# Count matrix of a four-layer graph network: 50 ranges of 50 destinations in place of 40 of 64, and an edge search in 28 places of 21 ranges

## The reference

```python
dst = min((2500 * uniform(40000) ** 2.0).astype(int32), 19999)   # then sorted, src with it
x = x + L0(h, ..., src, dst)                  # softmax over the edges into a node, sum of alpha * h[src]
W = zeros((256, 256)).at[rows, cols].set(w)   # L1: X @ W; rows = src, cols = dst, the last edge wins
agg = segment_sum(x[src], dst)                # L2: mean over neighbours, three times
x = x + L3(h, edge_index, W, a)
```

## Time and profile before

| | |
|---|---|
| median of 3 runs | 2108.89 us (2108.01 to 2110.15) |
| the profiled execution | 2108.91 us |
| its span | 2107.1 us |
| PE, DVE, ACT, POOL busy | 82%, 75%, 65%, 13% |
| block of the count matrix, first `ohc` to last `ohl` | 35.6 to 313.0 us |

### The profile page before, as it was taken

How to read it: one execution, slowest core, us unless ns; L and a number is a source line. 1 busy time by engine, 2 the same in 40 slices (tenths; PEclk the granted TensorE clock), 3 DMA queues, 4 the chain that set the end, 5 groups by cost and what they waited for, 6 DMA issues and landing times. The chain is left out here.

```text
span 2107.1 us, 63497 instructions
## 1 busy us (share of the span) xinstructions
PE 1724.7 (82%) x21987; PEld 1375.5 (65%) x21987; DVE 1575.6 (75%) x3485; ACT 1379.3 (65%) x2350; POOL 274.3 (13%) x421
## 2 busy tenths in 40 slices
PE   3999995598999748899893699998989985588883
PEld 1333333598888627889882477775558984588883
DVE  6999997899999888999999532222332257899996
ACT  0246794999999659999995622221113355799986
POOL 2466510366700000000000000000000000000000
PEclk9999997799999978999996899999999998799997
DMA  2000000011101000010101200000001010000002
GB/s 77 12 1 2 2 3 27 14 31 37 40 27 40 2 27 30 28 40 28 40 28 50 97 2 0 0 0 7 0 16 40 20 61 14 8 27 21 21 21 99
DMA packets 34789, 54.87 MB, mean 26 GB/s; under 512 B 10668, under 2 KB 26240, under 8 KB 34432
## 3 DMA queue, kind: packets, MB, share of 16 engines
q1 hardware_dynamic: 31232, 51.64, 7.5%
q0 software_dynamic: 3328, 0.06, 0.1%
HBM read 43.19 MB, written 8.49 MB: 25 GB/s over the span
## 5 line engine op out<-in xcount | busy, mean ns | idle before, releaser
L1069 ACT ACTIVATE Rm<-rows,cB 128x1280 bf16<-128x1280 f32 (+3 forms) x816 | 847.1, 1132 | 32.4 <-DVE Mn L1104 19.2
L1206 PE MATMUL ps<-R,M 128*128 128x132 f16 (+1 forms) x8640 | 684.1, 221 | 117.3 <-DVE Mn L1104 62.7
L1206 PEld LDWEIGHTS ps<-R,M 128*128 128x128 f16 x8640 | 545.4, 97 | 141.6 <-DVE M L1114 51.8
L1114 DVE TENSOR_TENSOR M<-Rm,C 128x1280 f16<-128x1280 bf16 (+3 forms) x816 | 527.9, 673 | 37.0 <-ACT Rm L1069 26.6
L1199 PE MATMUL ps<-HB,C 128*128 128x66 f16 x6400 | 304.2, 194 | 60.5 <-DVEq L1095 60.5
L1199 PEld LDWEIGHTS ps<-HB,C 128*128 128x128 f16 x6400 | 258.9, 98 | 60.7 <-DVEq L1095 60.7
L600 PE MATMUL acc<-ohc,ohl 128*128 128x420 f16 (+1 forms) x1161 | 246.0, 348 | 27.1 <-DVE ohl L564 23.9
L562 DVE TENSOR_SCALAR ohc<-cells,near 128x1280 f16<-128x1280 f16 x387 | 214.7, 555 | 27.9 <-PE acc L600 23.5
L1117 DVE SCALAR_TENSOR_TENSOR M<-rows,cN,C 128x1280 f16<-128x1280 f32 (+1 forms) x144 | 217.2, 1508 | 0.0
L600 PEld LDWEIGHTS acc<-ohc,ohl 128*128 128x128 f16 x1161 | 89.6, 98 | 175.6 <-DVE ohl L564 120.0
L1543 PE MATMUL psA<-R,C 128*128 128x512 f16 (+1 forms) x800 | 145.6, 332 | 8.1 <-DVEq L1827 3.2
(11 more groups left out here) (295 smaller groups left out, 2304.9 us busy)
## 6 DMA issues: line engine op xcount, KB each, us to landing
rows<-rowd SPq DMA_DIRECT2D x32, 640.0 KB, 3.9
rows<-rowd SPq DMA_DIRECT2D x16, 320.0 KB, 3.4
xd<-R SPq DMA_DIRECT2D x4, 640.0 KB, 2.9
xr<-xd SPq DMA_DIRECT2D x20, 128.0 KB, 2.1
xd<-HB SPq DMA_DIRECT2D x1, 2560.0 KB
xr<-xd SPq DMA_DIRECT2D x5, 512.0 KB, 6.4
R<-in_x SPq DMA_DIRECT2D x1, 2432.0 KB
xr<-in_x SPq DMA_DIRECT2D x19, 128.0 KB, 2.0
```

Source lines behind the costliest of these rows:

```text
L1069: a.activation(Rm[:, s % SG, 0:wide(p)], rows[:, p % 2, 0:wide(p)], ACT.Relu, bias=cB[:, ds(h + s * nh, 1)]).then_inc(s_R, 1)
L1114: v.tensor_tensor(M[:, u, 0:wide(p)], Rm[:, u, 0:wide(p)], Cs, ALU.min).then_inc(s_M if s in ONE else s_cut, 1)
L1206: m = pe.matmul(region(p % 2, r), lhsT, rhs, start=split and opens and r % 3 == 0, stop=True, skip_group_check=True)
```

## The change

- 50 ranges of 50 destinations (1000 cells). The banks are two of 500 columns. Destinations 2500 to 2559 belong to no range; POOL sets them to zero in the first block.
- A range's first two chunks (AHEAD) stand straight in the code, and the loop of threes comes behind them, with at least one turn. A range thus has 5, 8, 11, ... chunks in place of 6, 9, 12, ...; the ring's slot for a chunk is (2q + u) mod 3.
- The codes are shifted for two ranges at once (NEAR): `cells` has 2000 numbers, and an odd range compares with the second 1000.
- The search is in 28 places (NS): two one behind the other in each of ranges 0 to 6 and one in each of ranges 7 to 20, on PE after the two straight chunks. The number of searches at one place comes from the table (`turns`), up to 3.
- The chunks with dst < 256 are now taken from the first 6 ranges, thus up to destination 300.

```diff
-WW = 64
-NW = NP // WW
+WW = 50
+NW = -(-N // WW)
 U3 = 3
+AHEAD = 2
+NEAR = 2
...
+SEARCHED = [2] * 7 + [1] * 14
+NS = sum(SEARCHED)
+TURNS = -(-RND // NS)
...
-        DSPLIT = [(0, 22), (22, 43), (43, 64)]
-        cells = sb("cells", [P, CELLS], f16, edge)
+        DSPLIT = [(0, 25), (25, 50)]
+        cells = sb("cells", [P, NEAR * CELLS], f16, edge)
...
+                g.memset(C[:, :].rearrange("p (s d) -> p s d", d=NP)[:, :, NW * WW:NP], 0.0).then_inc(s_xz, 1)
...
-                ch(v.tensor_scalar(threes, threes, 1 / U3, 1 / U3, ALU.mult, ALU.add))
+                ch(v.tensor_scalar(threes, threes, 1 / U3, (1 - AHEAD) / U3, ALU.mult, ALU.add))
...
-                WT = D // WW
+                WT = -(-D // WW)
...
-                ch(v.tensor_scalar(table[:, T + 5:T + 6], many, 2.0 / NW, 0.5 - 1.0 / NW, ALU.mult, ALU.add))
+                ch(v.tensor_scalar(table[:, T + 5:T + 6], many, 2.0 / NS, 0.5 - 1.0 / NS, ALU.mult, ALU.add))
...
-                for q in range(NW):
+                for q in range(NS):
                     w = q % 2
                     with sp.Fori(0, turns) as i:
                         r = round_of(sp, q, i)
...
+                for q in range(NW):
+                    for c in searched(q):
+                        search(c)
...
-                    if q + 2 < NW:
-                        close_codes(q + 2)
+                    if q % NEAR == NEAR - 1 and q // NEAR + 2 < GROUPS:
+                        close_codes(q // NEAR + 2)
...
-                    v.wait_ge(s_near, q + 1)
+                    v.wait_ge(s_near, q // NEAR + 1)
+                    own = cells[:, q % NEAR * CELLS:(q % NEAR + 1) * CELLS]
+
+                    def one(i, u):
+                        k, w = chunk(first + i * U3 + u, NG * P - 1), slot_of(q, u)
+                        v.wait_ge(s_used, (before + i) * U3 + (q * AHEAD + u + 1))
+                        v.tensor_scalar(ohc[:, w, :], own, near[:, q // NEAR % 2, ds(k, 1)], None,
+                                        ALU.is_equal).then_inc(s_oh, 1)
...
+                    for u in range(AHEAD):
+                        one(0, u)
                     with v.Fori(0, threes) as i:
-                        for u in range(U3):
...
+                        for u in range(AHEAD, AHEAD + U3):
+                            one(i, u)
...
-                    three(0, True)
...
+                    for u in range(AHEAD):
+                        one(0, u, u == 0)
+                    for c in searched(q):
+                        search(c)
+                    with pe.Fori(0, threes) as i:
+                        for u in range(AHEAD, AHEAD + U3):
+                            one(i, u)
```

More of the change, by code:

```diff
@@ L117, in build @@
         hmax = sb("hmax", [P, NT], f32)
-        table = sb("table", [1, 4 * NW + 12], i32)
+        table = sb("table", [1, ROUNDS + TURNS * NS], i32)
         wd = nc.dram_tensor("wd", [D * D, 1], f32, kind="Internal").ap()
@@ L385, in _ @@
                 ch.wait()
[L386 to L388 removed]
+                for i in range(TURNS):
+                    ch(v.tensor_scalar(each[:, i, :], row[:, 4, 0:NS], turns, float(i), ALU.mult, ALU.add))
                 ch.wait()
[L390 removed]
+                ch(v.tensor_scalar(each[:, :, :], each[:, :, :], r1, r0, ALU.min, ALU.add))
                 ch.wait()
[L392 removed]
+                ch(v.tensor_copy(table[:, ROUNDS:ROUNDS + TURNS * NS].rearrange("a (i q) -> a i q", i=TURNS), each[:, :, :]))
                 ch(v.tensor_tensor(table[:, T + 3:T + 4], e0, some, ALU.add))
@@ L479, in threes_of, with slot_of, searched @@
             def threes_of(entry):
-                return nc.s_assert_within(entry // PACK, 2, NCH, skip_runtime_bounds_check_because=
-                                          "the table is built with at least two threes, and no more than cover NCH chunks")
+                return nc.s_assert_within(entry // PACK, 1, NCH, skip_runtime_bounds_check_because=
+                                          "the table is built with at least one three, and no more than cover NCH chunks")
+            def slot_of(q, u):
+                return (q * AHEAD + u) % U3
+            def searched(q):
+                return range(sum(SEARCHED[:q]), sum(SEARCHED[:q + 1]))
             @block.gpsimd
@@ L528, in _, with search @@
                 done = 0
-                for q in range(NW):
+                def search(c):
                     with a.Fori(0, turns) as i:
-                        n = turns * q + i
+                        n = turns * c + i
                         found = nc.s_assert_within(e0 + n * 4, 0, 8 * RND - 4, skip_runtime_bounds_check_because=
@@ L587, in _, with search @@
                 coming, before = packed(pe, 0), 0
+                def search(c):
+                    with pe.Fori(0, turns) as i:
+                        n = turns * c + i
+                        pe.wait_ge(s_sq, n + 1)
+                        hold(pe, s_row[c % 2], turns * (c // 2 * 48) + i * 48 + 48)
+                        pe.matmul(psD[c % 2][:, :], big16[:, :], notlater[:, :, :].rearrange("p u j -> p (u j)"),
+                                  start=True, stop=False)
+                        pe.matmul(psD[c % 2][:, :], left[:, c % 2, :], right[:, c % 2, :], start=False,
+                                  stop=True).then_inc(s_D, 1)
                 for q in range(NW):
@@ L591, in _ @@
                         coming = packed(pe, q + 1)
[L593 to L602, removed]
@@ L614, in _, with one @@
-                    with pe.Fori(1, threes) as i:
-                        three(i, False)
+                    def one(i, u, opening=False):
+                        w = slot_of(q, u)
+                        pe.wait_ge(s_oh, (before + i) * (2 * U3) + ((q * AHEAD + u) * 2 + 2))
+                        for b, (d0, d1) in enumerate(DSPLIT):
+                            if opening:
+                                pe.wait_ge(s_out, q * NB + b + 1)
+                            ins = pe.matmul(bank(b, q % 2), ohl[:, w, :], ohc[:, w, d0 * NT:d1 * NT],
+                                            start=opening, stop=True, skip_group_check=True)
+                        ins.then_inc(s_used, 1)
```

33 lines of the change are left out of this document (16 added, 17 removed).

## The result

The changed kernel takes 2124.19 us (median, 2123.39 to 2125.59) beside 2109.52 (2108.01 to 2110.49) of the kernel before, measured with it: a ratio of 1.0068 [1.0056, 1.0081], **14.7 us slower**. The forecast of 2119 had the direction, and the range from 2106 to 2129 holds the time. Two terms of its sum were wrong, and a gain was missing from it. The profiled execution has a span of 2122.0 us, 14.9 over the 2107.1 of before, so the two traces can be laid side by side.

A forecast was written before the change was run, and what follows sets the result against it. DVE's chunks were taken to set the pace of the count-matrix block. On 2108.9 us, -19.4 + 5.0 - 2.9 + 25.2 + 2.1 + 0.3 = +10.3 gave 2119 us; forecast's own range 2112 to 2126, wider range 2106 to 2129.

The forecast's parts named there:

- Shorter compare: DVE's compare on 1000 columns: 0.553 us a chunk for 403 chunks, against 0.626 for 387; -19.4 us.
- Range ends: DVE's pause at each range's end: 49 instead of 39, kept at 0.5 us each (bounds 0.1 and 0.65); +5.0 us.
- hidden by the straight chunks: Rival: two straight chunks fill DVE's queue before the loop, range-end pause shrinks to 0.1 us; 2099.5 us, chance 0.08.
- Single searches: DVE's pause behind a lone PE search: 13 of 0.47 us in place of 20 of 0.45; -2.9 us.
- Double searches: Ranges 0 to 6: PE waits 2.4 us for the second search's rows, DVE pauses 3.6 us; +25.2 us.
- The rival that the clock falls: PE's clock drops to 1.2 GHz in its 2.4 us pauses, adding some 25 us: 2144 us, chance 0.08.
- ACT: ACT is freed in ranges 21 to 49 and its shifts halved, but it hardly held DVE's pace; 0 us.
- First block: POOL's longer patterns, zeros and table rows delay PE's first transposes; +2.1 us (0.5 to 3).
- Scatters: POOL's later scatters, 48 in place of 40, stay hidden except beside a full DVE; +0.3 us (0 to 2).

The follow-up runs named there:

- e10_old_40: Kernel before (40 ranges of 64, one search in each), but each range's first three chunks stand straight, with the loop behind the search: 2103.61 us, ratio 0.9965.
- e1_spread: Changed kernel with one search in each of ranges 0 to 27 instead of two in 0 to 6 and one in 7 to 20: 2094.00 us, ratio 0.9925.
- e3_warm: Changed kernel with six extra PE matmuls, their results overwritten, between the two searches of ranges 0 to 6: 2115.41 us, ratio 1.0025.
- e2_ahead: Changed kernel, but SP loads a search's rows once the search before the last has ended, not the last one: 2109.62 us, ratio 0.9992.
- e4_load_late: Changed kernel, but DVE loads the next range's table entry after its two straight chunks, not ahead of them: 2116.94 us, ratio 1.0029.

## Why the prediction was right in direction and short in size

1. *Shorter compare*, -19.4: right. 0.5535 us a chunk against 0.553 forecast, -18.9 in all. The slope between two forms of one operation was a good price.
2. *Range ends*, +5.0: wrong by 5.5 us. The step was "I keep 0.5, since the load of the entry and the first address stay". They stay, but the branch into the loop leaves, and an end costs 0.37 over the pace as the mean, in e10_old_40 0.35 with nothing else changed. I had read this in the order of the instructions and given it no price. The truth lay between the bounds 0.1 and 0.65, and the rival "hidden by the straight chunks" (0.1) was no nearer than my 0.5.
3. *Single searches*, -2.9: e1_spread bears out that a single search costs little: ranges 0 to 6 lose 8.8 us for seven of them and the start of the block. The term itself was not measured apart.
4. *Double searches*, +25.2, of which the share over single searches was 3.1 each or 22: measured 34.2 in the ranges concerned, 28 to 30 in the whole time. The gap's 2.4 us was right to a tenth. "The pause is 0.47 + 2.4 + 0.7 = 3.6" failed, since it let PE go on at full speed behind the gap. The pauses are 4.1 to 4.75 us, and the chunks behind them are slow. Where e3_warm keeps the clock up, the pause is 3.4 to 3.7 over the pace and a double search costs 3.2 more than a single one: both as forecast, so the wait was priced well and the clock was what it lacked. The rival that the clock falls had the mechanism, and the earlier trace rows showed its level; I gave it 0.08 with the argument that 2.4 us is short beside the 12 in that row. It is not exclusive of the forecast, as I had it, but adds to it: 9 to 11 us, not the 25 that I gave it. The Trainium skill, "TensorE: Matmul & The Clock Gate", section "Part 1: The HAM clock gate", says that an idle array goes back to half its clock; the 0.53 of this trace from 123 to 126 us agrees. The row of before had the lower level behind 12 us of standing, and could not tell what 2.4 us would do.
5. *ACT*, 0: nothing contradicts it. In e2_ahead, once the rows are there, ACT's square is what ends the gap.
6. *First block*, +2.1: 1.7 measured. The memset is 1.13 us and the longer pattern 0.60 more.
7. *Scatters*, +0.3: not told apart; the rest of the program moved by less than its own spread.
8. *Missing from the sum:* the handover to the next block, -3.5. I looked at the searches only where they stand in PE's way and not at who waits for the last of them. The last ranges still had their searches before, the one that ends at 299 among them; POOL's last operation waited for the last of all, and DVE's 4.25 us behind the block was in the trace, unread.

The sum with the measured sizes: -18.9 - 0.5 + 34.2 + 1.7 - 3.5 = +13.0, and +1.9 in the rest. The Trainium skill, "DMA: Bandwidth & Descriptors", section "Anatomy of one DMA — SWDGE (gpsimd) path", fits about 2.0 us of fixed cost, for transfers that GpSimd issues. Carried over to SP's, it would have given a gap of 3.0; the trace has 2.34 to 2.81, so here the lower figure from the rows was the better one. The errors (+5.5 too dear, 3.5 missed, 12 too cheap) partly made up for each other, which is why 2119 looks better than its steps.

Where does the gain of the shorter compare go, then? Not into contention, and not off the critical path: the runs show that it is there (e1_spread, 2094.0). The seven double searches take it and 11 us more. The runs let the cost be divided, by what ranges 1 to 6 lose over the chunks' pace in each trace, as the mean of a range: 6.0 in the changed kernel, 4.2 in e3_warm where the clock holds, 3.0 in e2_ahead where the clock holds (ranges 2, 4 and 5), 1.0 in e1_spread. Of the 5.0 that a double search costs over a single one, 1.8 are thus the clock, 1.2 the part of the wait for the rows that outlasts ACT's square, and 2.0 the second search behind the first with the square between them. This is from one trace of each kernel, and no run had both edits. The 14.6 us that e2_ahead gives back are the second part and much of the first, since a shorter wait also spares the clock.

## What to carry to other kernels

When steps that wait for memory are moved together, price not the steps but the gap between them: who issues the next load, behind what, and what the waiting engine does in it. A gap of PE costs its length and, where the clock falls in it, the slow matmuls behind it. Work that has slack inside a block (here 28 searches over 50 ranges) is best spread one to a place and finished early, so that what hangs on the last of it, here another engine's drain, is over when the block ends.

## What the runs showed of the hardware that I had not expected

- The granted clock fell in or behind PE's pauses of 2.34 to 2.81 us in ranges 1 to 6 of the changed kernel (range 0 was low already). Behind pauses of 1.19 us it fell in three of these six ranges (e2_ahead), and behind 0.94 us in two (e3_warm, at 115.64 and 129.03); in the others it held. It did not fall behind single searches (1.00 from 37 to 134 us in e1_spread).
- POOL's drain at the end of its block stands in the trace for 6.5 us, before (315.38 to 321.86) and after (269.75 to 276.25), though its last operation takes only 1.1.
- The entry of a loop with a count from memory costs DVE an empty 0.12 to 0.15 us (e4_load_late), and a table load with its set-up about 0.3 (0.40 less 0.11), between two instructions that have no data to wait for. The profile puts the end of such a pause down to PE, which had long been done.
